# Attention scores with the query halves kept in their own partitions: three products on 64-row tiles, two head pairs at a time

## The chip, the cores and the metric

The kernel runs on one core of one Trainium2 chip. The metric is the device time of one launch in microseconds (us). The kernel before takes 839.48 us, the median of three runs (838.78 to 839.79).

## The reference, cut to what matters

The input `x` is (8, 512, 512): eight rows of 512 tokens and 512 features. Each row attends to its own 64 context tokens (16 heads of 32 features), is projected and added back, and then goes through a gated feed-forward layer with ternary weights and quantised activations. Only the scores are touched by the change.

```python
q = _nan_clean(proj(hs, Wq, bq, S))
k = _nan_clean(proj(at, Wk, bk, T))
v = _nan_clean(proj(at, Wv, bv, T))
scale = max(math.sqrt(HD), 1e-08)
scores = jnp.einsum('bhsd,bhtd->bhst', q, k) / scale
scores = jnp.clip(scores, -50.0, 50.0)
...
scores = jnp.where(attend, scores, -10000.0)
scores = jnp.clip(scores, -50.0, 50.0)
probs = jax.nn.softmax(scores, axis=-1)
...
ctx = jnp.einsum('bhst,bhtd->bhsd', probs, v)
```

Queries and keys are float32 numbers held as two float16 parts, a high one (the number rounded) and a low one (what is left), so that TensorE can multiply them as float16.

## The kernel before

**The work.** A row of `x` is four tiles of 128 tokens. `body(b, ...)` does the feed-forward of row b and, in its gaps, the attention of row a = b + 1 and the layer norm of row c = b + 2. It is called for b = -1 to 8: b = 1 to 5 are a hardware loop, the others straight code. "Body 3" below is the call with b = 3. Scores are computed in the eight bodies b = -1 to 6, once each. Inside a body, t runs over the four token tiles: at t = 0 the queries of row a are made, at t = 1 its scores, at t = 2 the weighted values, and at t = 3 the projection begins. The order on each engine is written out by hand and every dependence is a semaphore: a wait holds up all that stands behind it on its engine.

**Queries, t = 0.** On TensorE (PE), `query(m)` (L1447) makes 128 features, that is four heads, with twelve matmuls in one of the two PSUM banks `psA`. On ScalarE (ACT), `query(m)` (L729) copies the bank, scaled, to `q_whole` (L740), and then writes the high part in two copies (L743, L744): partitions 0 to 63 (two heads) into slot 2m of `q_parts` and partitions 64 to 127 (the other two) into slot 2m + 1, each staying in its partitions. On VectorE (DVE), `q_low` (L959) writes the low part of each half (L964, L965) into the other half of the partitions of the same slot. A slot has thus 64 rows of high and 64 rows of low parts of the same two heads.

**Scores, t = 1.** `scores(j)` on PE (L1459) makes a pair of heads with two matmuls of 128 rows by 512 tokens (L1470, L1471): high keys against both parts of the query, then low keys against both. The keys of a row stand in `kcur`, loaded from a scratch tensor by `load_keys` (L416) with eight DMAs; in each slot they are laid out block by block with zeros, so that one head's keys fill 64 of the 128 output rows. On ACT, `exps` (L746) turns each finished bank into exponentials (L749). The banks alternate:

```python
if j >= 2:
    wait(pe, p_ready, a, j - 1)
```

so that the product of one pair is made in one bank while ACT reads the other. Between scores, PE does parts of `down` (L1430), the output matrix of the feed-forward of the tile before, by the table `BETWEEN_SCORES` (L1655): 12 of its 16 matmuls (L1435). The last 4 stand behind `project`. ACT rounds the next tile's input (L709) between the second and the third exponential.

**Behind the scores.** PE does two transposes (L1410, L1378) and the projection (L1444, thirteen matmuls), whose bank is free once the last exponential is done. ACT copies the transposed layer norm (`h_high`, L679) behind its last exponential. DVE then does `h_low` (L970), four clips of the exponentials (`bound`, L1077), the statistics of the projection (L1018), and, at t = 2, the gated products (L983, L988) with the attention output (L1083, L1088, L1096) between them.

Of the kernel before, what the change touches and what calls it, by code (L numbers as in the profile page):

```python
# [17 lines left out]
F16 = mybir.dt.float16  # L18
# [6 lines left out]
P = 128  # L25
# [34 lines left out]
def build(nc, x, ctx_in, mask, g_x, g_f, Wq, bq, Wk, bk, Wv, bv, Wo, bo, ln_g, ln_b, res_scale,  # L60
# [18 lines left out]
    with es:  # L79
# [47 lines left out]
        q_parts = room(6).bitcast(F16).rearrange("p (j s) -> p j s", j=NPAIR)  # L127
# [49 lines left out]
        kcur = sb("kcur", [P, 2 * NPAIR, 2 * T], F16)  # L177
# [105 lines left out]
        k_loaded = per_row("keys_loaded", 16 * 2 * HPC)  # L283
# [112 lines left out]
        def _(sp):  # L396
# [19 lines left out]
            def load_keys(row):  # L416
                wait_alone(sp, s_met_sp, sc_done, row - 1, NPAIR)
                for i in range(HPC):
                    for q in range(2):
                        e = i % 2  # L420
                        head = HD * (2 * q + e)
                        sp.dma_start(kcur[HD * i:HD * (i + 1), q::2, e * T:(e + 1) * T],
                                     k_dram[head:head + HD, :, row, :]).then_inc(k_loaded.sem, 16)
# [223 lines left out]
        def _(act):  # L647
# [34 lines left out]
            def body(b, prev, ffn, att, pre):  # L682
# [46 lines left out]
                def query(m):  # L729
                    wait(act, q_done, a, m + 1)  # L730
                    if b is FIRST and m == 0:
                        act.wait_ge(s_vmax, 1)
                    if ffn and not prev and m == 0:
                        act.wait_ge(s_wabs, 3 * W_CHUNKS)
                    if m < 2:
                        wait(act, c_tr, b, NT)
                    else:
                        wait(act, ql_ready, a, m - 1)
                    whole = q_whole[:, m % 2, :]
                    A.activation(whole, psA[(m + 1) % 2][:], ACT.Identity, scale=down_q[:, 0:1],  # L740
                                 bias=bq_c[:, m:m + 1]).then_inc(qT_ready.sem, 1)
                    wait(act, qT_ready, a, m + 1)
                    A.copy(q_parts[0:P // 2, 2 * m, :], whole[0:P // 2, :])  # L743
                    A.copy(q_parts[P // 2:, 2 * m + 1, :], whole[P // 2:, :]).then_inc(qh_ready.sem, 1)  # L744
# [135 lines left out]
        def _(dve):  # L880
# [78 lines left out]
            def q_low(row, m):  # L959

                wait(dve, qh_ready, row, m + 1)
                one, other = slice(0, P // 2), slice(P // 2, P)
                whole = q_whole[:, m % 2, :]
                V.tensor_tensor(q_parts[other, 2 * m, :], whole[one, :], q_parts[one, 2 * m, :], ALU.subtract)  # L964
                V.tensor_tensor(q_parts[one, 2 * m + 1, :], whole[other, :], q_parts[other, 2 * m + 1, :],  # L965
# [377 lines left out]
        def _(pe):  # L1343
# [39 lines left out]
            def body(b, prev, ffn, att, pre):  # L1383
# [75 lines left out]
                def scores(j):  # L1459
                    if j == 0:  # L1460
                        wait(pe, ql_ready, a, KC)
                        wait(pe, k_loaded, a, 16 * 2 * HPC)
                        if pre:
                            wait(pe, lo_ready, c, 1)
                    if j == 1:
                        wait(pe, d_ready, b, 3)
                    if j >= 2:
                        wait(pe, p_ready, a, j - 1)

                    M.matmul(psA[(j + 1) % 2][:], kcur[:, j, :], q_parts[:, j, :], start=True, stop=False)  # L1470
                    M.matmul(psA[(j + 1) % 2][:], kcur[:, NPAIR + j, :], q_parts[:, j, :],  # L1471
                             start=False, stop=True).then_inc(sc_done.sem, 1)
# [45 lines left out]
                for t in range(NT):  # L1518
# [46 lines left out]
                    if att and t == 1:  # L1565
                        if out_w_now:
                            pe.wait_ge(s_wcopy, 3 * W_GROUPS)
                        for j in range(NPAIR):
                            scores(j)
                            if finish and j in BETWEEN_SCORES:  # L1570
                                down(*last, BETWEEN_SCORES[j])
# [83 lines left out]
BETWEEN_SCORES = {1: range(0, 5), 2: range(5, 6), 3: range(6, 9), 4: range(9, 10), 5: range(10, 11), 6: range(11, 12)}  # L1655
AFTER_SCORES = 12
# [23 lines left out]
```

## Time and profile before

| | |
|---|---|
| median of 3 runs | 839.48 us (838.78 to 839.79) |
| the profiled execution | 841.52 us, span 839.7 us |
| mean granted TensorE clock | 0.970 of full |
| DMA | 50.90 MB, 61 GB/s |
| instructions | 14590 |

The span runs from the first to the last instruction. One body of the loop takes some 88 us of it. The profile gives for each engine the time in which an instruction ran; on PE, matmuls follow each other before the earlier one has ended, so the distance between two starts is what one costs in a stream and its duration is what one costs alone.

### The profile page before, as it was taken

Reading aid. Unit: us, or ns where it says so; the run is one execution under the profiler, and the core shown is the slowest. Engines: PE = TensorE matmul, PEld = TensorE weight load, DVE = VectorE, ACT = ScalarE, POOL = GpSimd, SP = SyncE. Lnnn points to the kernel's source line nnn. Section 1 sums busy time; section 2 is a strip of 40 time slices with the busy share of each in tenths; the row PEclk is TensorE's granted clock in tenths of the full one; section 3 lists DMA queues with packets and bytes.
Section 4 is the critical chain, followed back from the end, with each engine's and each line's share of the span. In section 5 each row is a group of like instructions: output and inputs, shape, how many; then the busy total and the mean of one; then the engine's idle time right before and its main releaser. Section 6 shows DMA issues by size and latency. Waiting matters only on the chain.

```text
span 839.7 us, 14590 instructions
## 1 busy us (share of the span) xinstructions
PE 750.2 (89%) x4886; PEld 384.6 (46%) x4886; DVE 697.7 (83%) x1412; ACT 534.0 (64%) x693; POOL 240.2 (29%) x427
## 2 busy tenths in 40 slices
PE   4695658969999999999999999999999999999995
PEld 4442344434544454445444544454445444454442
DVE  6778876898889888888988988988888888779982
ACT  4447858767557755784578557855676556745563
POOL 4101003221333324232433333314422332223431
PEclk9898768999999999999999999999999999999998
DMA  8572345101030103011211121111111020001000
GB/s 275 192 261 64 130 165 170 26 14 39 2 95 10 42 26 77 17 37 37 56 37 37 37 52 42 37 37 42 51 37 37 17 52 26 26 2 51 13 26 26
DMA packets 51663, 50.90 MB, mean 61 GB/s; under 512 B 30877, under 2 KB 30877, under 8 KB 50857
## 3 DMA queue, kind: packets, MB, share of 16 engines
q1 hardware_dynamic: 51624, 50.42, 19.2%
q8 instruction: 21, 0.34, 0.2%
q14 instruction: 18, 0.14, 0.1%
HBM read 39.91 MB, written 10.50 MB: 60 GB/s over the span
## 4 chain that ended last, share of the span: by engine, by line
PE 45%; DVE 31%; issue 11%; ACT 10%; POOL 1%; DMA 1%; DVEq 0%; POOLq 0%; ACTq 0%
PE psum L1444 14%; PE psum L1399 13%; PE psum L1435 7%; DVE arena L988 4%; DVE psum L983 3%; ACT arena L749 2%; DVE arena L1088 2%; PE psum L1402 2%; PE psum L1427 2%; PE psum L1378 2%; DVE xmax L1060 1%; DVE arena L1096 1%; PE psum L1470 1%; DVE stats L1048 1%; DVE arena L922 1%
## 5 line engine op out<-in xcount | busy, mean ns | idle before, releaser
L1399 PE MATMUL psum<-ternary,xqT 128*128 128x512 f16 x1024 | 261.3, 379 | 2.8 <-DVE xqT L1009 2.6
L554 POOL TENSOR_TENSOR rstd<-var_e,minus_half 128x1 f32<-128x1 f32 x64 | 40.0, 625 | 406.5 <-DVE var_e L1028 263.9
L1399 PEld LDWEIGHTS psum<-ternary,xqT 128*128 128x128 f16 x1024 | 96.3, 98 | 108.3 <-DVE xqT L1009 3.5
L1435 PE MATMUL psum<-ternary,arena 128*128 128x512 f16 x512 | 128.0, 383 | 1.2 <-ACT arena L726 1.2
L693 ACT ACTIVATE arena<-psum,dequant 128x512 f32<-128x512 f32 x128 | 87.2, 682 | 43.2 <-PE psum L1402 42.8
L983 DVE SCALAR_TENSOR_TENSOR psum<-psum,dequant,valb_b 128x512 f32<-128x512 f32 x128 | 96.3, 752 | 20.2 <-PE psum L1399 19.7
L988 DVE TENSOR_TENSOR arena<-psum,arena 128x512 f32<-128x512 f32 x128 | 88.5, 692 | 20.8 <-ACT arena L693 17.1
L1444 PE MATMUL psum<-wo_hi,arena 128*128 128x512 f16 x256 | 84.4, 392 | 2.5 <-DVE arena L1096 1.9
L1444 PE MATMUL psum<-arena,wq_hi 128*128 128x512 f16 x256 | 77.5, 385 | 7.1 <-ACT arena L740 7.1
L726 ACT ACTIVATE arena<-psum,round_c 128x1024 f16<-128x1024 f16 x64 | 71.3, 1114 | 19.1 <-PE psum L1427 18.7
L701 ACT ACTIVATE arena<-arena,round_c,hscale 128x1024 f32<-128x1024 f32 x64 | 75.9, 1236 | 4.6 <-DVE hscale L1004 4.4
L992 DVE TENSOR_REDUCE hmax<-arena 128x1 f32<-128x1024 f32 x64 | 77.6, 1213 | 0.7
L1435 PEld LDWEIGHTS psum<-ternary,arena 128*128 128x128 f16 x512 | 48.9, 99 | 57.4 <-ACT arena L726 4.4
L1444 PE MATMUL psum<-wo_lo,arena 128*128 128x512 f16 x128 | 50.1, 391 | 0.0
L586 POOL TENSOR_TENSOR arena<-arena 128x512 f32<-128x512 f32 x32 | 42.2, 1319 | 25.2 <-ACT arena L721 25.2
L1444 PE MATMUL psum<-arena,wq_lo 128*128 128x512 f16 x128 | 49.2, 384 | 0.0
L1402 PE MATMUL psum<-bias_parts,inv_rows 128*128 128x512 bf16 x128 | 48.5, 379 | 0.0
L749 ACT ACTIVATE arena<-psum,scur 128x512 f32<-128x512 f32 x64 | 46.5, 775 | 1.2 <-PE psum L1471 0.5
L714 ACT CAST inv_rows<-psum 128x128 bf16<-128x128 f32 x32 | 8.6, 269 | 57.7 <-DVE xqT L1009 57.7
L740 ACT ACTIVATE arena<-psum,bq_c,down_q 128x512 f32<-128x512 f32 x32 | 24.9, 777 | 30.4 <-PE psum L1444 28.9
L709 ACT ACTIVATE arena<-x_both,round_c,xscale 128x512 f32<-128x512 f32 x32 | 25.9, 810 | 27.8 <-DVE xscale L1070 27.7
L1492 PE MATMUL psum<-vcur,arena 128*64 128x66 f32 x1024 | 38.3, 229 | 5.8 <-DVE delta L1033 4.4
(181 smaller groups left out, 1348.7 us busy)
## 6 DMA issues: line engine op xcount, KB each, us to landing
arena<-in_x SPq DMA_DIRECT2D x64, 256.0 KB, 2.7
out<-arena SPq DMA_DIRECT2D x32, 256.0 KB, 2.0
arena<-in_L_ffn_gate_w SPq DMA_DIRECT2D x4, 1024.0 KB, 10.0
arena<-in_L_ffn_out_w SPq DMA_DIRECT2D x3, 1024.0 KB, 9.6
ternary<-in_L_ffn_val_w SPq DMA_DIRECT2D x2, 1024.0 KB, 10.2
kcur<-k_scratch SPq DMA_DIRECT2D x64, 32.0 KB, 2.2
ternary<-in_ctx SPq DMA_DIRECT2D x1, 1024.0 KB, 5.4
ternary<-in_L_xattn_Wk SPq DMA_DIRECT2D x1, 1024.0 KB, 8.0
```

The source lines that it names most:

```text
L586: G.tensor_tensor(resid[:, t, :], resid[:, t, :], y_part[:, t % 2, :], ALU.add).then_inc(y_ready.sem, 1)
L693: A.activation(gs[:, t % 2, n * CW:(n + 1) * CW], psG[n % 2], ACT.Silu, scale=dequant[:, t, 0:1]).then_inc(silu_done.sem, 1)
L701: A.activation(gs[:, t % 2, cols], gs[:, t % 2, cols], ACT.Identity, scale=hscale[:, t:t + 1], bias=round_c[:, 0:1]).then_inc(hq_ready.sem, 1)
L726: A.activation(hidT[:, h * FC // 2:(h + 1) * FC // 2, :].rearrange("p k n -> p (k n)"), half(psO), ACT.Identity, bias=round_c[:, 1:2]).the ...
L749: A.activation(probs[:, j, :], psA[(j + 1) % 2][:], ACT.Exp, scale=scur[:, 0:1], bias=scur[:, 1:2]).then_inc(p_ready.sem, 1)
L983: V.scalar_tensor_tensor(out=psV[n % 2], in0=psV[n % 2], scalar=dequant[:, t, 1:2], in1=valb_b[:, n * CW:(n + 1) * CW], op0=ALU.mult, op1= ...
L988: V.tensor_tensor(part, psV[n % 2], part, ALU.mult).then_inc(hid_ready.sem, 1)
L992: V.tensor_reduce(hmax[:, t, h:h + 1], gs[:, t % 2, h * F // 2:(h + 1) * F // 2], AX, ALU.max, apply_absolute_value=True).then_inc(hm_read ...
L1399: ins = M.matmul(ps[:], xqT[:, t % 2, k, :], w[:, k, cols], start=(k == 0), stop=(w is wv and k == KC - 1))
L1402: ins = M.matmul(ps[:], inv_rows[:, t % 2, :], bias_parts[:, cols], start=False, stop=True)
L1435: ins = M.matmul(psO[:], hidT[:, k, :], wo2[:, k, :], start=(k == 0), stop=(k == FC - 1))
L1444: ins = M.matmul(ps[:], lhsT, rhs, start=(n == 0), stop=(n == len(pairs) - 1))
```

## The change

`q_parts` becomes four-dimensional (part, m, token): all 128 partitions of the high part lie in one place and all of the low part in another, so nothing crosses partitions. ACT writes the high part with one copy for each m, DVE the low part with one subtraction. `kcur` is laid out in the same way, with four DMAs for each row of `x`. `scores(m)` takes the place of two calls of `scores(j)`: six matmuls, each on 64 of the 128 rows, in turn on the lower half (two heads, bank `psA[1]`) and on the upper half (the next two, bank `psA[0]`): high keys by high query, high by low, low by high. The product of the low parts is left out.

```diff
-        q_parts = room(6).bitcast(F16).rearrange("p (j s) -> p j s", j=NPAIR)
+        q_parts = room(6).bitcast(F16).rearrange("p (two m s) -> p two m s", two=2, m=KC)
...
-        kcur = sb("kcur", [P, 2 * NPAIR, 2 * T], F16)
+        kcur = sb("kcur", [P, 2, KC, 2 * T], F16)
...
                 for i in range(HPC):
-                    for q in range(2):
-                        e = i % 2
-                        head = HD * (2 * q + e)
-                        sp.dma_start(kcur[HD * i:HD * (i + 1), q::2, e * T:(e + 1) * T],
-                                     k_dram[head:head + HD, :, row, :]).then_inc(k_loaded.sem, 16)
+                    e, head = i % 2, slice(HD * i, HD * (i + 1))
+                    sp.dma_start(kcur[head, :, :, e * T:(e + 1) * T].rearrange("p two m t -> p (two m) t"),
+                                 k_dram[head, :, row, :]).then_inc(k_loaded.sem, 16)
...
                     wait(act, qT_ready, a, m + 1)
-                    A.copy(q_parts[0:P // 2, 2 * m, :], whole[0:P // 2, :])
-                    A.copy(q_parts[P // 2:, 2 * m + 1, :], whole[P // 2:, :]).then_inc(qh_ready.sem, 1)
+                    A.copy(q_parts[:, 0, m, :], whole).then_inc(qh_ready.sem, 1)
...
                 wait(dve, qh_ready, row, m + 1)
-                one, other = slice(0, P // 2), slice(P // 2, P)
-                whole = q_whole[:, m % 2, :]
-                V.tensor_tensor(q_parts[other, 2 * m, :], whole[one, :], q_parts[one, 2 * m, :], ALU.subtract)
-                V.tensor_tensor(q_parts[one, 2 * m + 1, :], whole[other, :], q_parts[other, 2 * m + 1, :],
+                V.tensor_tensor(q_parts[:, 1, m, :], q_whole[:, m % 2, :], q_parts[:, 0, m, :],
                                 ALU.subtract).then_inc(ql_ready.sem, 1)
...
-                def scores(j):
-                    if j == 0:
+                def scores(m):
+                    if m == 0:
                         wait(pe, ql_ready, a, KC)
-                        wait(pe, k_loaded, a, 16 * 2 * HPC)
+                        wait(pe, k_loaded, a, 16 * HPC)
                         if pre:
                             wait(pe, lo_ready, c, 1)
-                    if j == 1:
                         wait(pe, d_ready, b, 3)
-                    if j >= 2:
-                        wait(pe, p_ready, a, j - 1)
-
-                    M.matmul(psA[(j + 1) % 2][:], kcur[:, j, :], q_parts[:, j, :], start=True, stop=False)
-                    M.matmul(psA[(j + 1) % 2][:], kcur[:, NPAIR + j, :], q_parts[:, j, :],
-                             start=False, stop=True).then_inc(sc_done.sem, 1)
+                    else:
+                        wait(pe, p_ready, a, 2 * m)
+
+                    for n, (of_k, of_q) in enumerate(((0, 0), (0, 1), (1, 0))):
+                        for e in range(2):
+                            pair = slice(e * 2 * HD, (e + 1) * 2 * HD)
+                            ins = M.matmul(psA[(e + 1) % 2][:], kcur[pair, of_k, m, :], q_parts[pair, of_q, m, :],
+                                           start=(n == 0), stop=(n == 2))
+                            if n == 2:
+                                ins.then_inc(sc_done.sem, 1)
...
-BETWEEN_SCORES = {1: range(0, 5), 2: range(5, 6), 3: range(6, 9), 4: range(9, 10), 5: range(10, 11), 6: range(11, 12)}
-AFTER_SCORES = 12
+BETWEEN_SCORES = {0: range(0, 5), 1: range(5, 10), 2: range(10, 15)}
+AFTER_SCORES = 15
```

How the instructions stand, at two places. The first is PE in body 0 at t = 1, from the first product of the scores on (L1470 and L1471 are the two products of a pair, L1435 is `down`; `exp_ready` is the semaphore `p_ready`). Before:

```order
L1470 MATMUL psum<-arena,kcur 128x512 [waits keys_loaded,hT_low_ready,query_low_ready,weight_copied]
L1471 MATMUL psum<-arena,kcur 128x512
L1470 MATMUL psum<-arena,kcur 128x512 [waits delta_ready]
L1471 MATMUL psum<-arena,kcur 128x512
L1435 MATMUL psum<-ternary,arena 128x512 [waits hidT_ready]
L1435 MATMUL psum<-ternary,arena 128x512 x4
L1470 MATMUL psum<-arena,kcur 128x512 [waits exp_ready]
L1471 MATMUL psum<-arena,kcur 128x512
L1435 MATMUL psum<-ternary,arena 128x512
L1470 MATMUL psum<-arena,kcur 128x512 [waits exp_ready]
L1471 MATMUL psum<-arena,kcur 128x512
L1435 MATMUL psum<-ternary,arena 128x512 x3
```

In the changed kernel, from the same place to the transposes (L1466 is the product, L1429 is `down`, L1404 the first transpose):

```order
L1466 MATMUL psum<-arena,kcur 128x512 [waits hT_low_ready,keys_loaded,delta_ready,query_low_ready,weight_copied]
L1466 MATMUL psum<-arena,kcur 128x512 x5
L1429 MATMUL psum<-ternary,arena 128x512 [waits hidT_ready]
L1429 MATMUL psum<-ternary,arena 128x512 x4
L1466 MATMUL psum<-arena,kcur 128x512 [waits exp_ready]
L1466 MATMUL psum<-arena,kcur 128x512 x5
L1429 MATMUL psum<-ternary,arena 128x512 x5
L1466 MATMUL psum<-arena,kcur 128x512 [waits exp_ready]
L1466 MATMUL psum<-arena,kcur 128x512 x5
L1429 MATMUL psum<-ternary,arena 128x512 x5
L1466 MATMUL psum<-arena,kcur 128x512 [waits exp_ready]
L1466 MATMUL psum<-arena,kcur 128x512 x5
```

The groups that wait for exponentials are three instead of six, and each stands for two pairs and waits for the exponentials of both pairs before it. Fifteen `down` matmuls stand in the gaps instead of twelve.

The second place is DVE in body 0 at t = 0, where the low parts of the query are made (L964 and L965), between the work of the feed-forward (L983, L988, L992) and of a weight's clipping (L922). Before:

```order
L992 TENSOR_REDUCE hmax<-arena 128x1
L964 TENSOR_TENSOR arena<-arena 64x512
L965 TENSOR_TENSOR arena<-arena 64x512
L983 SCALAR_TENSOR_TENSOR psum<-psum,dequant,valb_b 128x512
L988 TENSOR_TENSOR arena<-psum,arena 128x512
L922 TENSOR_SCALAR arena<-arena 128x2048
L964 TENSOR_TENSOR arena<-arena 64x512
L965 TENSOR_TENSOR arena<-arena 64x512
```

In the changed kernel (L959 is the low part, L986 is the reduction, L977 and L982 the feed-forward, L919 the clipping):

```order
L986 TENSOR_REDUCE hmax<-arena 128x1
L959 TENSOR_TENSOR arena<-arena 128x512
L977 SCALAR_TENSOR_TENSOR psum<-psum,dequant,valb_b 128x512
L982 TENSOR_TENSOR arena<-psum,arena 128x512
L919 TENSOR_SCALAR arena<-arena 128x2048
L959 TENSOR_TENSOR arena<-arena 128x512
```

One instruction on 128 partitions stands where two on 64 stood, and nothing else has moved.

## Rows read from the trace of the kernel before

**Rows 1.** The page: busy time of the engines, us (share of the span).
```profile
PE 750.2 (89%) x4886; PEld 384.6 (46%) x4886; DVE 697.7 (83%) x1412; ACT 534.0 (64%) x693; POOL 240.2 (29%) x427
```
**Rows 2.** Body 3 in five stretches: busy us of each engine, granted clock, DMA.
```profile
413.80:451.00 37.20, 37.20 (x203) 18.27 (x202) 32.58 (x68) 26.33 (x36) 11.67 (x17) 1.00 0.16 48
451.00:459.10 8.10, 7.92 (x40) 3.03 (x37) 7.00 (x16) 7.96 (x11) 3.75 (x9) 1.00 0.00 0
...
465.65:484.00 18.35, 17.30 (x209) 11.04 (x210) 17.16 (x38) 8.03 (x13) 5.68 (x11) 1.00 0.12 43
```
**Rows 3.** Timeline, scores of body 3, ACT and DVE: start, us, engine, line.
```profile
451.31 1.28 ACT L749 ACT_TABLE_LOAD   x1
452.61 1.45 ACT L749 ACTIVATE arena<-psum,scur 128x512 f32<-128x512 f32 x2
453.95 0.81 ACT L709 ACTIVATE arena<-x_both,round_c,xscale 128x512 f32<-128x512 f32 x1
454.66 4.40 ACT L749 ACTIVATE arena<-psum,scur 128x512 f32<-128x512 f32 x6
459.20 0.59 ACT L679 CAST arena<-psum 128x512 f16<-128x512 f32 x1
...
459.82 0.69 DVE L970 TENSOR_TENSOR arena<-psum,arena 128x512 f16<-128x512 f32 x1 [0.84 <-ACT arena L679]
```
**Rows 4.** Timeline of the same stretch, PE and its weight loads.
```profile
451.27 0.38 PE L1470 MATMUL psum<-arena,kcur 128*128 128x512 f16 x1
451.49 0.38 PE L1471 MATMUL psum<-arena,kcur 128*128 128x512 f16 x1
...
453.44 0.10 PEld L1470 LDWEIGHTS psum<-arena,kcur 128*128 128x128 f16 x1 [0.56 <-ACT arena L749]
```
**Rows 5.** Groups by form: busy us, mean ns of one, idle before.
```profile
L965 DVE TENSOR_TENSOR arena<-arena 64x512 f16<-64x512 f32 x32 | 22.0, 687 | 0.4
L970 DVE TENSOR_TENSOR arena<-psum,arena 128x512 f16<-128x512 f32 x32 | 21.9, 684 | 8.5 <-ACT arena L679 8.5
L744 ACT CAST arena<-arena 64x512 f16<-64x512 f32 x32 | 19.7, 615 | 0.4
L749 ACT ACTIVATE arena<-psum,scur 128x512 f32<-128x512 f32 x64 | 46.5, 775 | 1.2 <-PE psum L1471 0.5
```
**Rows 6.** The chain that ended last, in body 0: start, us, engine, line.
```profile
149.87 0.62 ACT arena L744
...
156.72 0.68 DVE arena L964
157.42 0.69 DVE arena L965
...
198.89 0.86 PE psum L1435 x4
```
**Rows 7.** Timeline of body -1, where the clock is low; ACT and PE.
```profile
84.40 0.62 ACT L744 CAST arena<-arena 64x512 f16<-64x512 f32 x1
...
95.07 0.63 PE L1471 MATMUL psum<-arena,kcur 128*128 128x512 f16 x1
95.49 0.63 PE L1470 MATMUL psum<-arena,kcur 128*128 128x512 f16 x1
...
95.80 1.57 ACT L749 ACTIVATE arena<-psum,scur 128x512 f32<-128x512 f32 x2
101.58 1.44 ACT L749 ACTIVATE arena<-psum,scur 128x512 f32<-128x512 f32 x2
```
**Rows 8.** Timeline, PE: matmuls on 64 output columns (L1492) and on whole tiles.
```profile
465.65 1.16 PE L1492 MATMUL psum<-vcur,arena 128*64 128x66 f32 x32 [0.75 <-DVE delta L1033]
52.33 10.55 PE L1627 MATMUL psum<-ternary 128*128 128x512 f32 x24
```
**Rows 9.** Timeline of body 0: the table load waits for the first score.
```profile
188.12 1.28 ACT L749 ACT_TABLE_LOAD   x1 [1.95 <-PE psum L1471]
```
**Rows 10.** Timeline of the DMA queue: issue of the keys for body 3.
```profile
410.13 3.94 SPq L422 DMA_DIRECT2D kcur<-k_scratch  x6
```

More of the change, by code:

```diff
@@ L282, in build @@
         xt_loaded = [per_row(f"xt{i}_loaded", 16 * NT // 2) for i in range(2)]
-        k_loaded = per_row("keys_loaded", 16 * 2 * HPC)
+        k_loaded = per_row("keys_loaded", 16 * HPC)
         v_loaded = per_row("values_loaded", 16 * 2)
@@ L1567, in body @@
                             pe.wait_ge(s_wcopy, 3 * W_GROUPS)
[L1568 to L1571, printed above, removed]
+                        for m in range(KC):
+                            scores(m)
+                            if finish and m in BETWEEN_SCORES:
+                                down(*last, BETWEEN_SCORES[m])
                     if finish and not (att and t == 1):
```

## The prediction

> **What bounds the kernel now.** I read the busy times, then one body of the loop in stretches, then the timeline inside the stretch that the change touches, and last the chain of waits for the bodies that differ. PE is busy for 89% of the span and DVE for 83% [rows 1]; such averages do not say which of the two a saving must come from. The stretches do [rows 2]. From 413.8 to 451.0 us (queries, first gate products) PE is busy for all of 37.20 us, with DVE at 32.58 and ACT at 26.33: a PE stretch. From 451.0 to 459.1 (the scores) ACT is busy for 7.96 of 8.10 us. PE shows 7.92 there too, but its busy time counts a matmul to its end; its weight loads show real stops, such as 0.56 us before a score, released by ACT's exponential [rows 4]. From 465.65 to 484.0 DVE carries the time, 17.16 of 18.35.
>
> The scores are the place to look at closely [rows 3]: a table load at 451.31, two exponentials, the rounding at 453.95, six exponentials in one run of 4.40 us from 454.66, the copy L679 at 459.20. ACT never stops. It does not, because the banks alternate: PE makes pair j + 1 while ACT reads pair j. And all that follows waits for this run: DVE stands idle for 0.84 us before L970 at 459.82, released by L679, so DVE has no backlog to hide a later end in, and the projection needs the last exponential as well.
>
> **The change, part by part.** Differences within 0.2% (1.7 us) I call the same.
>
> *High and low parts of the queries.* ACT loses one of two copies for each m, 615 ns; DVE one of two subtractions, 687 ns. The ones that stay take 128 partitions instead of 64, at the same 512 elements in each: the 128-partition subtraction L970 takes 684 ns [rows 5], so they cost no more than one half did. That is 32 of each, 22.0 us of DVE and 19.7 us of ACT in all. In bodies 1 to 6 it lies under PE's unbroken 37 us: **0**. The cover is PE, and no other work is queued late at its end, since ACT and DVE both wait for something in the score stretch. In body 0 the weights are still being clipped on DVE and the chain runs through both subtractions of all four m (156.72 and 157.42 are the first two) and through one copy at 149.87 [rows 6]: -4 x 0.69 - 0.62 = **-3.4 us**, at least 0 if another engine takes over at once. In body -1, two ACT copies (84.40 is one) and one subtraction stand in the same kind of chain ahead of the scores [rows 7]: -0.62 x 2 - 0.69 = **-1.9 us**.
>
> *Key loads.* Four DMAs instead of eight. Those for body 3 are issued from 410.13 [rows 10] and read at 451.27 [rows 4]: 41 us early. **0**, either way.
>
> *The scores.* Two products of a pair start 0.22 us apart [rows 4], so 16 full products are 3.5 us of PE. The new 24 on 64 rows are 12 x 0.22 = 2.6 us if the two halves of the array work at once, and 5.2 us if not. No row shows 64-row tiles. The nearest are 64-column ones: 32 float32 matmuls of 66 columns start and end in 1.16 us, 0.036 us each, while 24 of 512 columns take 10.55 us, 0.44 us each, which for 66 columns would be 0.057 us [rows 8]. Two such tiles do overlap, so I take the halves as concurrent and keep the serial price as the other end.
>
> What matters is the wait. `scores(m)` needs **both** banks, so it needs both exponentials of the two pairs before. PE cannot make the next scores under an exponential any more, and ACT stands still from the end of one pair of exponentials until the fifth of six products has ended. From exponential to PE 0.05 us (452.61 + 0.78 = 453.39, load at 453.44 [rows 3 to 5]); two steps of 0.22 to the fifth start; 0.38 to its end [rows 4]; 0.05 back to ACT: 0.91 us. Walking through body 3:
> - exponentials 0 and 1 start at 452.61 as before, since the table load covers the longer first group (451.27 + 0.43 + 0.38 = 452.08), and end at 454.06;
> - 2 and 3: 454.06 + 0.91 = 454.97, not 454.66. The rounding covers the rest. They end at 456.42;
> - 4 and 5: start at 457.33, end at 458.78;
> - 6 and 7: start at 459.69, end at **461.14**, against 454.66 + 4.40 = 459.06 before.
>
> That is **+2.1 us a body**. Queued behind it are h_low, the clips and the statistics on DVE, L679 and the quantisation on ACT, and the projection on PE; all of them move. For seven bodies (0 to 6): **+14.6**. In bodies 0 and 6 the table load itself waits for the first score [rows 9], which now ends one step later: **+0.4** together. In body -1 the clock is at its lower level, steps are 0.42 us and a product 0.63 [rows 7], and the layer norm stands ahead of the last two exponentials. The run from 95.80 to 103.02 (101.58 + 1.44) would grow by 0.4 before its first exponential, by some 1.5 at the second group, 0.9 at the third (clock back up) and little at the fourth, less 0.35 of waits that it has already: **+2.4**.
>
> *`down`.* Three more of its matmuls lie in gaps where PE waits for ACT: 5 x 0.22 = 1.1 us after 0.65 us of scores end before the exponentials do (1.45 + 0.91 from one group to the next). Behind the projection 1 is left instead of 4. In bodies 1 to 6 DVE comes there from its clips and is last: 0. In body 0 the four are on the chain [rows 6]: **-0.6**.
>
> **Sum:** -3.4 - 1.9 + 14.6 + 0.4 + 2.4 - 0.6 = **+11.5 us**, against a profiled execution of 841.5 us (span 839.7). The median of the runs is 2.0 us under that execution; the difference carries over, so 839.5 + 11.5 = **851.0 us**.
>
> Two rules speak on the score term. The rows gave a gap by the wait alone. The Trainium skill, TensorEngine Tiling (Array Packing), PSUM Bottleneck, says that tiling speeds up TensorE and not the emptying of PSUM; the 7.96 of 8.10 us of ACT [rows 2] agree, and by that rule alone the change would give 0 in the score stretch and not a loss, a result of 833.6. The same page, Key Properties, says that a change of tiling mode drains TensorE; no row here shows such a change between row tilings. As an estimate, a drain of 0.16 us (a product's 0.38 less its step of 0.22) at each group would be hidden where PE waits anyway.
>
> **Rivals.**
> 1. *The halves run one after the other.* The fifth product then starts 0.86 us after the first, and each gap is 1.34 us: per body +0.4 at the second group and +0.43 at each of the last two, 3.4 us instead of 2.1; +0.9 more in bodies 0 and 6, +2.5 in body -1. Sum: 11.5 + 9.1 + 0.9 + 2.5 = +24, **863.5 us**. For it: nothing in the rows shows two row tiles at once. Against: the column tiles overlap [rows 8]. 0.17.
> 2. *The relief is worth more than the gap* (faster). If the late part of DVE's work in a body began earlier by its 2.75 us for four subtractions, the loss of 2.1 would turn into -0.65 a body: -4.6 for seven, and with -3.4, -1.9, -0.6, +0.4 and +2.4 about **832 us**. It decides where DVE has no idle time between t = 0 and L970. DVE's 32.58 of 37.20 us and its 0.84 us wait speak against it [rows 2, 3]. 0.04.
> 3. *The score stretch costs nothing* and only the relief is left, as the emptying rule has it: PE would have to start a group ahead of the second exponential, which the wait forbids. -3.4 - 1.9 - 0.6 = **833.6 us**. 0.03.
> 4. *The clock falls.* PE now stops for some 0.5 to 1 us three times in the stretch. If the granted clock, 1.00 in all of body 3 [rows 2], dropped to its lower level for the 2.8 us of the projection in each of seven bodies, that adds 2.8 x 7 = 20 us: **871 us**. PE was busy the stretch before and is again right after. 0.03.
>
> **How the numbers follow.** My forecast has 0.73 and its own range is 848 to 855: body 0's relief may be 0 instead of 3.4, and the terms of body -1 are rough by 2 us. The predicted time is its time. To hold 8 in 10 the range goes down to 846 and up over the serial case to 865. Faster: rivals 2 and 3, 0.07. The same: 0.02, a mixture of a smaller gap and more relief. Slower: 0.91.
>
> **What would show it.** In the changed profile: 32 whole-width copies near 0.62 us and 32 subtractions near 0.69; in each looped body ACT idle twice by about 0.9 us before an exponential, released by PE, with one run of six split into three pairs; pairs of products starting within a few hundredths of a microsecond of each other (rival 1: 0.22 apart); L679 of body 3 2.1 us later after the table load than now (7.9 us); the loop's bodies at 90 us instead of 88, and bodies -1 and 0 together shorter or level. The forecast is wrong if ACT still runs its exponentials without a stop, or if the stretch is longer and the body is not.

## The result, and the profile after

| | before | after |
|---|---|---|
| median of the runs, us | 839.63 (838.78 to 840.45, 4 runs) | 849.73 (848.55 to 850.84, 4 runs) |
| profiled execution, us | 841.5 | 848.55 |
| its span, us | 839.7 | 846.8 |
| mean granted clock of the span | 0.97 | 0.97 |

The ratio is 1.012, with a 95% interval from 1.0101 to 1.0139. The changed kernel is slower by 10.1 us, and its time lies 1.3 us under the predicted 851.0.

The page of the changed kernel, its busy times (to set beside [rows 1]) and two groups, then the groups by form (beside [rows 5]; columns: busy us, mean ns of one, idle time before and what ended it):

```profile
PE 742.3 (88%) x4888; PEld 382.9 (45%) x4950; DVE 667.4 (79%) x1380; ACT 511.1 (60%) x661; POOL 237.8 (28%) x427
L746 ACT ACTIVATE arena<-psum,scur 128x512 f32<-128x512 f32 x64 | 46.3, 773 | 17.0 <-PE psum L1466 16.9
L1466 PE MATMUL psum<-arena,kcur 64*128 64x512 f16 x192 | 26.9, 387 | 19.3 <-ACT arena L746 16.7
```

```profile
L959 DVE TENSOR_TENSOR arena<-arena 128x512 f16<-128x512 f32 x32 | 23.5, 739 | 0.0
L741 ACT CAST arena<-arena 128x512 f16<-128x512 f32 x32 | 19.8, 618 | 1.0
```

DVE lost 30 us of busy time and ACT 23, and the kernel is slower. The reason stands in the idle column of L746: the exponentials, which waited 1.2 us in all before, now wait 17.0, for the scores; and the scores wait 16.7 of their 19.3 for the exponentials. The two engines take turns where they used to overlap. The timeline of ACT in the score stretch of body 3 shows it (beside [rows 3]; columns: start us, us, engine, line, count, in brackets the idle time before the group and what ended it):

```profile
451.14 1.28 ACT L746 ACT_TABLE_LOAD   x1
452.44 1.45 ACT L746 ACTIVATE arena<-psum,scur 128x512 f32<-128x512 f32 x2
453.78 0.81 ACT L707 ACTIVATE arena<-x_both,round_c,xscale 128x512 f32<-128x512 f32 x1
454.80 1.45 ACT L746 ACTIVATE arena<-psum,scur 128x512 f32<-128x512 f32 x2 [0.21 <-PE psum L1466]
457.15 1.44 ACT L746 ACTIVATE arena<-psum,scur 128x512 f32<-128x512 f32 x2 [0.91 <-PE psum L1466]
459.51 1.45 ACT L746 ACTIVATE arena<-psum,scur 128x512 f32<-128x512 f32 x2 [0.91 <-PE psum L1466]
461.11 0.58 ACT L677 CAST arena<-psum 128x512 f16<-128x512 f32 x1
```

One run of six has become three pairs. From the first exponential to the end of the last it is 460.96 - 452.44 = 8.52 us, against 459.06 - 452.61 = 6.45 before: +2.07. The same stretch on PE, beside [rows 4]:

```profile
451.20 0.82 PE L1466 MATMUL psum<-arena,kcur 64*128 64x512 f16 x6
451.95 1.25 PE L1429 MATMUL psum<-ternary,arena 128*128 128x512 f16 x5
453.94 0.82 PE L1466 MATMUL psum<-arena,kcur 64*128 64x512 f16 x6 [0.74 <-ACT arena L746]
454.69 1.25 PE L1429 MATMUL psum<-ternary,arena 128*128 128x512 f16 x5
456.30 0.82 PE L1466 MATMUL psum<-arena,kcur 64*128 64x512 f16 x6 [0.35 <-ACT arena L746]
```

Six products start and end in 0.82 us, which is two steps of 0.22 and one duration of 0.38: three pairs side by side. Even the five `down` matmuls between two groups leave PE standing for 0.35 us. DVE waits longer for the copy behind the last exponential, 1.40 us instead of 0.84 [rows 3]:

```profile
461.72 0.69 DVE L964 TENSOR_TENSOR arena<-psum,arena 128x512 f16<-128x512 f32 x1 [1.40 <-ACT arena L677]
```

**Where the time went.** The two profiled executions, piece by piece; the marks are the table loads L749/L746 ahead of the exponentials, which start at 188.12, 275.50, 363.51, 451.31, 539.08, 626.84 and 714.80 before, and at 182.17, 271.65, 361.40, 451.14, 540.89, 630.63 and 720.89 after (bodies 0 to 6).

| piece | before, us | after, us | difference | by the prediction's terms |
|---|---|---|---|---|
| start to the rounding L662/L660, ahead of any changed work | 67.75 | 65.86 | -1.9 | 0 |
| from there to the first exponential of body -1 | 28.05 | 24.45 | -3.6 | -1.9 |
| from it to the copy L679/L677 behind the last | 7.30 | 9.68 | +2.4 | +2.4 |
| from there to the table load of body 0 | 85.02 | 82.18 | -2.8 | -3.4 + 0.2 |
| table load of body 0 to that of body 6 | 526.68 | 538.72 | +12.0 | 6 x 2.1 + 0.2 - 0.6 |
| from there to the end of the span | 124.9 | 125.9 | +1.0 | +2.1 |

Together +7.1, the difference of the spans. The first row is no effect of the change; without it the sum is +9.0. The medians of the runs differ by 10.1, so this pair of executions shows about 3 us less than the runs do; the table is for the pieces, not for the total.

### The profile page after: what moved, and what is told of

The parts are those of the page before. It is cut to its first block, busy times and chain, and to the rows that moved or that the text cites. A ratio compares the mean times of both kernels' runs of the same rounds, so it can differ in the third digit from the quotient of the medians.

```text
span 846.8 us, 14525 instructions
## 1 busy us (share of the span) xinstructions
PE 742.3 (88%) x4888; PEld 382.9 (45%) x4950; DVE 667.4 (79%) x1380; ACT 511.1 (60%) x661; POOL 237.8 (28%) x427
## 4 chain that ended last, share of the span: by engine, by line
PE 41%; DVE 32%; ACT 13%; issue 11%; POOL 1%; DMA 1%; DVEq 0%; POOLq 0%; another core or an unknown queue 0%; ACTq 0%; SPq 0%
PE psum L1438 13%; PE psum L1393 12%; PE psum L1429 6%; ACT arena L746 4%; DVE arena L982 4%; DVE psum L977 4%; PE psum L1466 3%; DVE arena L1082 2%; DVE hmax L986 2%; PE psum L1372 2%; DVE xmax L1054 1%; PE psum L1421 1%; DVE arena L1071 1%; ACT arena L699 1%; DVE arena L1090 1%
## 5 line engine op out<-in xcount | busy, mean ns | idle before, releaser
L1393 PE MATMUL psum<-ternary,xqT 128*128 128x512 f16 x1024 | 261.3, 379 | 5.5 <-DVE xqT L1003 1.5
L1393 PEld LDWEIGHTS psum<-ternary,xqT 128*128 128x128 f16 x1024 | 96.4, 98 | 107.0 <-DVE arena L982 3.1
L1429 PE MATMUL psum<-ternary,arena 128*128 128x512 f16 x512 | 124.8, 383 | 1.6 <-ACT arena L724 1.2
L977 DVE SCALAR_TENSOR_TENSOR psum<-psum,dequant,valb_b 128x512 f32<-128x512 f32 x128 | 96.2, 752 | 29.4 <-PE psum L1393 29.4
L982 DVE TENSOR_TENSOR arena<-psum,arena 128x512 f32<-128x512 f32 x128 | 88.5, 691 | 21.4 <-ACT arena L691 17.6
L986 DVE TENSOR_REDUCE hmax<-arena 128x1 f32<-128x1024 f32 x64 | 77.6, 1213 | 0.7
L1429 PEld LDWEIGHTS psum<-ternary,arena 128*128 128x128 f16 x512 | 47.2, 99 | 61.3 <-issue 11.1
L746 ACT ACTIVATE arena<-psum,scur 128x512 f32<-128x512 f32 x64 | 46.3, 773 | 17.0 <-PE psum L1466 16.9
L738 ACT ACTIVATE arena<-psum,bq_c,down_q 128x512 f32<-128x512 f32 x32 | 24.8, 776 | 43.7 <-PE psum L1438 43.2
L1489 PE MATMUL psum<-vcur,arena 128*64 128x66 f32 x1024 | 40.0, 236 | 8.9 <-DVE delta L1027 7.5
L1489 PEld LDWEIGHTS psum<-vcur,arena 128*64 128x64 f32 x1024 | 35.7, 148 | 22.0 <-issue 14.8
L558 POOL TENSOR_TENSOR arena<-arena,beta_b 128x512 f32<-128x512 f32 x32 | 44.4, 1388 | 0.0
L1466 PE MATMUL psum<-arena,kcur 64*128 64x512 f16 x192 | 26.9, 387 | 19.3 <-ACT arena L746 16.7
```

What stands on the lines that cost most here:

```text
L746: A.activation(probs[:, j, :], psA[(j + 1) % 2][:], ACT.Exp, scale=scur[:, 0:1], bias=scur[:, 1:2]).then_inc(p_ready.sem, 1)
L977: V.scalar_tensor_tensor(out=psV[n % 2], in0=psV[n % 2], scalar=dequant[:, t, 1:2], in1=valb_b[:, n * CW:(n + 1) * CW], op0=ALU.mult, op1= ...
L982: V.tensor_tensor(part, psV[n % 2], part, ALU.mult).then_inc(hid_ready.sem, 1)
L986: V.tensor_reduce(hmax[:, t, h:h + 1], gs[:, t % 2, h * F // 2:(h + 1) * F // 2], AX, ALU.max, apply_absolute_value=True).then_inc(hm_read ...
L1393: ins = M.matmul(ps[:], xqT[:, t % 2, k, :], w[:, k, cols], start=(k == 0), stop=(w is wv and k == KC - 1))
L1429: ins = M.matmul(psO[:], hidT[:, k, :], wo2[:, k, :], start=(k == 0), stop=(k == FC - 1))
```

## The experiments

Each kernel ran beside the kernel before on the same chip. That took 840.31 us (839.06 to 842.86) beside four of them (the wait alone, the first with four banks, pair by pair, the halves) and 840.91 (838.47 to 842.45) beside the other four. Line numbers shift by a few from kernel to kernel.

### Is it the wait? The old products under the new wait

The kernel before, two 128-row products a pair, made to wait for both exponentials of the two pairs before:

```diff
-                    if j >= 2:
-                        wait(pe, p_ready, a, j - 1)
+                    if j >= 2 and j % 2 == 0:
+                        wait(pe, p_ready, a, j)
```

> The kernel before, with one thing changed: an even pair of heads waits for the exponentials of both pairs before it (p_ready, j) instead of for its own bank. No 64-row tile, no relief of DVE or ACT. Gap theory: at pairs 4 and 6 ACT stops for 0.05 + 0.22 + 0.38 + 0.05 = 0.70 us where it ran on with an overlap of 0.05, at pair 2 the rounding covers all but 0.1 us: +1.6 us a body, seven bodies +11.2, body -1 some +1.5: about 852 us. Rival, that the loss of the change comes from the tiled products (their drains, their issue) or from the table of down: no change, 839.6 us.

Measured: 853.48 us (851.59 to 854.09), 1.0157 (1.0141 to 1.0173). ACT in body 3:

```profile
459.67 1.45 ACT L749 ACTIVATE arena<-psum,scur 128x512 f32<-128x512 f32 x2
461.82 1.45 ACT L749 ACTIVATE arena<-psum,scur 128x512 f32<-128x512 f32 x2 [0.70 <-PE psum L1471]
463.96 1.45 ACT L749 ACTIVATE arena<-psum,scur 128x512 f32<-128x512 f32 x2 [0.70 <-PE psum L1471]
```

Nothing but a wait was changed, no product, copy or subtraction, and the kernel is slower by 13 us, more than the change itself. The gap is one product step shorter than the change's 0.91, because a pair is ready after two products. The loop's period is 89.22 us against 87.78: +1.44. So of the change's +2.07 a body, 1.44 is the wait and 3 x 0.21 = 0.63 the third product, one step at each of the three later groups.

### And the other way: the new products without the wait

The change with four banks for the scores. Pairs 2, 3, 6 and 7 go to the two banks of the gate products, which are free in that stretch in all bodies but body -1:

```diff
+        def scores_bank(b, j):
+            return (psG if j // 2 % 2 and b is not FIRST else psA)[(j + 1) % 2]
...
-                    else:
+                    elif b is FIRST:
                         wait(pe, p_ready, a, 2 * m)
+                    elif m == 1:
+                        wait(pe, silu_done, b, 2 * NCH)
+                    else:
+                        wait(pe, p_ready, a, 2 * m - 2)
```

> The changed kernel with the scores of m = 1 and 3 in the two banks of the gate (free by then) instead of in the same two, except in body -1: m = 1 waits for the last silu, m = 2 and 3 for the exponentials of m = 0 and 1. The products stay six at a time on both halves. Gap theory: ACT's exponentials run without a stop from the first to the last in bodies 0 to 6 as before the change, 6.45 us from the first start to the last end against 8.52 now: 849.7 - 7 x 2.1 = 835 us, under both kernels. Rival, that something else than the gap holds the stretch (PE's drains, DVE): 845 to 850 us.

Measured: 836.56 us (835.58 to 837.93), 0.9952 (0.9938 to 0.9966). ACT in body 3:

```profile
450.25 2.89 ACT L750 ACTIVATE arena<-psum,scur 128x512 f32<-128x512 f32 x4
453.64 1.45 ACT L750 ACTIVATE arena<-psum,scur 128x512 f32<-128x512 f32 x2 [0.49 <-PE psum L1474]
```

The gap of 0.21 and the first of 0.91 are gone, one of 0.49 is left ahead of the last two exponentials, and the loss has turned into a gain. The rest is a matter of the table: three groups of five `down` matmuls (1.1 us each) now keep PE from running ahead. With the table of `down` spread over all four groups of scores:

```diff
-BETWEEN_SCORES = {0: range(0, 5), 1: range(5, 10), 2: range(10, 15)}
-AFTER_SCORES = 15
+BETWEEN_SCORES = {0: range(0, 6), 1: range(6, 10), 2: range(10, 12), 3: range(12, 14)}
+AFTER_SCORES = 14
```

> The version with four banks, and a table of down that brings the last scores forward: 6, 4, 2 and 2 of down's matmuls behind the four groups, 2 left. In its trace ACT still stops for 0.49 us before the last two exponentials of a body, because ten down matmuls stand ahead of the last group on PE. With that gap gone: seven bodies x 0.49 = 3.4 us less than with the first table, about 833 us against 840.3 before. If the stop had another cause it stays, 836.6 us.

Measured: **834.22 us** (832.70 to 835.22), 0.992 (0.9904 to 0.9936): faster than both kernels. ACT in body 3:

```profile
446.27 1.45 ACT L750 ACTIVATE arena<-psum,scur 128x512 f32<-128x512 f32 x2
447.61 0.81 ACT L711 ACTIVATE arena<-x_both,round_c,xscale 128x512 f32<-128x512 f32 x1
448.31 4.23 ACT L750 ACTIVATE arena<-psum,scur 128x512 f32<-128x512 f32 x6
```

The unbroken run of six is back, 4.23 us instead of 4.40. The loop's period is 87.50 us against 87.78 before: 0.17 of it is the shorter run, and 0.11 is what the halved kernel below shows for the relief in the loop. So without the wait, and with this table, the change is worth 6.7 us by the medians. The spans of the two profiled executions differ by 7.2; 1.2 of that stands ahead of any changed work. Of the other 6.0, 4.0 lie between there and the table load of body 0, 1.6 from that to the table load of body 6, and 0.4 behind it. Whether the shorter run of exponentials would come to the kernel before as well, if it had four banks, was not tried.

### Half of the wait: pair by pair

The change with the scores asked for pair by pair (three products on one half of the array, waiting for the exponential before last, as before the change), and with the old table of `down`:

```diff
-                    else:
-                        wait(pe, p_ready, a, 2 * m)
+                    if j >= 2:
+                        wait(pe, p_ready, a, j - 1)
```

> The changed kernel with the scores made pair by pair in turn in the two banks, each waiting for its own bank only, three products of 64 rows one after the other, and the down table of the kernel before. The halves of the array then work in turn. Gap theory: from the end of an exponential to the next one in the same bank 0.05 + 0.43 + 0.38 + 0.05 = 0.91 us, in which the other bank's exponential runs 0.73: a gap of some 0.2 us at five pairs, 1.0 us a body instead of 2.1, and less in body -1: about 849.7 - 8 = 842 us. Rival, that the two halves at once are what saves time and the wait costs little: slower than the change, over 852 us.

Measured: 846.11 us (845.80 to 847.07), 1.0066 (1.005 to 1.0082): a miss by 4 us. Five lines of PE and three of ACT say why:

```profile
449.83 0.83 PE L1467 MATMUL psum<-arena,kcur 64*128 64x512 f16 x6
450.59 1.25 PE L1429 MATMUL psum<-ternary,arena 128*128 128x512 f16 x5
...
454.48 0.82 PE L1467 MATMUL psum<-arena,kcur 64*128 64x512 f16 x3
455.23 0.39 PE L1429 MATMUL psum<-ternary,arena 128*128 128x512 f16 x1
455.55 0.82 PE L1467 MATMUL psum<-arena,kcur 64*128 64x512 f16 x3
```

```profile
455.34 0.78 ACT L746 ACTIVATE arena<-psum,scur 128x512 f32<-128x512 f32 x1 [0.73 <-PE psum L1467]
456.41 0.78 ACT L746 ACTIVATE arena<-psum,scur 128x512 f32<-128x512 f32 x1 [0.30 <-PE psum L1467]
457.48 0.78 ACT L746 ACTIVATE arena<-psum,scur 128x512 f32<-128x512 f32 x1 [0.30 <-PE psum L1467]
```

A single pair's three products take as long as six of two pairs, 0.82 us, and what follows them starts 0.75 us after the first. With one `down` matmul behind them, 0.32 us more, PE comes to a new pair every 1.07 us, and between these groups it does not stop for ACT: here PE sets the pace, and ACT's 0.78 + 0.30 a pair only follows. The expectation had counted the wait for the bank and not PE's own time. The three `down` matmuls ahead of pair 4 hold that pair back further, 0.73. What the array gains by working in halves is had only where both halves have a free bank at the same moment.

### Does the third product cost its step? A fourth one

The change with the product of the low parts put back:

```diff
-                    for n, (of_k, of_q) in enumerate(((0, 0), (0, 1), (1, 0))):
+                    for n, (of_k, of_q) in enumerate(((0, 0), (0, 1), (1, 0), (1, 1))):
```

> The changed kernel with the product of the two low parts put back: eight matmuls for each m instead of six, on both halves in turn. Gap theory: each gap between pairs of exponentials grows by one step of 0.22 us, from 0.91 to 1.13 and from 0.21 to 0.43: +0.65 us a body, eight bodies +5.2, and 0.4 more where the table load waits for the first score. Against the kernel before +10.1 + 5.6, about 855.8 us. Rival, that PE's work and not the gap is what costs: PE has 8 x 0.22 = 1.7 us more a body, mostly in time in which it waits, so no change, or the whole +14 us, 864 us, if it stood on PE's path.

Measured: 856.79 us (855.76 to 858.31), 1.0193 (1.0175 to 1.0211). ACT and PE in body 3:

```profile
460.16 1.45 ACT L746 ACTIVATE arena<-psum,scur 128x512 f32<-128x512 f32 x2 [0.43 <-PE psum L1466]
462.74 1.45 ACT L746 ACTIVATE arena<-psum,scur 128x512 f32<-128x512 f32 x2 [1.13 <-PE psum L1466]
```

```profile
461.67 1.04 PE L1466 MATMUL psum<-arena,kcur 64*128 64x512 f16 x8 [0.35 <-ACT arena L746]
```

Each gap grew by one step: 0.43, 1.13 and 1.13, where it was 0.21, 0.91 and 0.91; eight products take 1.04. The loop's period rises by 0.65, three steps. Rival 1 of the prediction would have shown 0.43 a gap.

### Are the halves at work together only because they alternate?

The change with each group's products in another order, three on the lower half, then three on the upper:

```diff
-                    for n, (of_k, of_q) in enumerate(((0, 0), (0, 1), (1, 0))):
-                        for e in range(2):
+                    for e in range(2):
+                        for n, (of_k, of_q) in enumerate(((0, 0), (0, 1), (1, 0))):
```

> The changed kernel with the six products in another order: three on the lower half of the array, then three on the upper. Same waits. If two halves run at once only because the order alternates, the group now takes 1.46 us instead of 0.82. Gap theory: the first bank of the group is finished by its third product at 0.43 + 0.38 = 0.81 us, as before, and the second at 1.46, before the first exponential has ended (0.81 + 0.05 + 0.73), so ACT's gaps stay at 0.91 and 0.21 and the time stays at 849.7 to 850.5 us. PE's group and five down matmuls then fill 2.4 us, the whole distance of 2.36 between two groups, so up to +0.1 us at two gaps of a body, +1.4 in all. Rival, that concurrency of the halves is what the time hangs on: +0.65 us at each of three gaps, +14 us, 864 us.

Measured: 849.21 us (848.24 to 851.58), 1.011 (1.0087 to 1.0132), the change's own time within the noise. PE in body 3:

```profile
454.67 0.83 PE L1466 MATMUL psum<-arena,kcur 64*128 64x512 f16 x6 [0.73 <-ACT arena L746]
455.43 1.25 PE L1429 MATMUL psum<-ternary,arena 128*128 128x512 f16 x5
```

In a row the six would have taken 5 x 0.22 + 0.38 = 1.48 us, and the next matmul would have started 1.3 us after the first; it starts after 0.76. So three products that stand behind three others in the program ran beside them. The first line of the pair-by-pair kernel shows the same, since its pairs 0 and 1 are also written one after the other.

### What is the relief worth? Half-width copies and subtractions in the change

The change with the copy and the subtraction of each m cut into two halves again, as many instructions as before the change:

```diff
-                    A.copy(q_parts[:, 0, m, :], whole).then_inc(qh_ready.sem, 1)
+                    A.copy(q_parts[0:P // 2, 0, m, :], whole[0:P // 2, :])
+                    A.copy(q_parts[P // 2:, 0, m, :], whole[P // 2:, :]).then_inc(qh_ready.sem, 1)
```

The subtraction in `q_low` is cut in the same way.

> The changed kernel with the high and the low part of the query again written by two instructions of 64 partitions each. If the relief is worth what was forecast (3.4 us in body 0, 1.9 in body -1, nothing in the others): 849.7 + 5.3 = 855.0 us. If it is worth more, because body -1 came 5.5 us earlier in the changed trace: up to 858. If it is worth nothing: 849.7 us. In bodies 1 to 5 the distance from one table load to the next stays at 89.8 us under the first two.

Measured: 858.54 us (856.52 to 859.11), 1.0208 (1.0191 to 1.0224). By the medians the relief is worth 8.8 us, or 8.1 if each kernel is set against the runs of the kernel before that were taken beside it, and not 5.3. The period of the loop is 89.86 against 89.75: the cover that the prediction named, PE's 37 us, holds but for 0.11. Most of the relief sits in the two other bodies. The way from the rounding L660 to the first exponential of body -1 is 94.42 - 66.23 = 28.19 us, as before the change (28.05), against 24.45; and from the copy L677 of body -1 to the table load of body 0 it is 190.12 - 105.41 = 84.71, near the 85.02 of before, against 82.18. These are 3.7 and 2.5 us. The spans of the two profiled executions differ by 9.9. Of the rest, 1.3 is the score stretch of body -1, 10.99 us here against 9.68; that is not the relief, since two kernels that have the relief show 10.88 (the first with four banks) and 10.99 (the one with 12 `down` matmuls, below), with the clock at 0.50 in most of it. 0.4 stands ahead of any changed work, 0.8 from the table load of body 0 to that of body 6, and 1.2 behind that, with no cause shown. ACT in body -1, of the kernel before, of the change, and of this one:

```profile
82.96 0.78 ACT L740 ACTIVATE arena<-psum,bq_c,down_q 128x512 f32<-128x512 f32 x1 [0.97 <-DVE arena L965]
...
93.23 0.59 ACT L679 CAST arena<-psum 128x512 f16<-128x512 f32 x1 [1.98 <-PE psum L1378]
```

```profile
80.00 0.76 ACT L738 ACTIVATE arena<-psum,bq_c,down_q 128x512 f32<-128x512 f32 x1
...
87.92 0.58 ACT L677 CAST arena<-psum 128x512 f16<-128x512 f32 x1 [1.16 <-PE psum L1372]
...
90.31 1.44 ACT L746 ACTIVATE arena<-psum,scur 128x512 f32<-128x512 f32 x2
```

```profile
81.31 0.78 ACT L738 ACTIVATE arena<-psum,bq_c,down_q 128x512 f32<-128x512 f32 x1 [0.85 <-DVE arena L962]
...
91.43 0.59 ACT L677 CAST arena<-psum 128x512 f16<-128x512 f32 x1 [1.82 <-PE psum L1375]
```

Whole-width work takes away three things: the wait of ACT for the subtractions (0.97), two copies, and some 0.8 us of the wait for the transposes behind them. PE comes to these sooner after its last work (it had stood still for 1.06 us in the change, for 2.46 us in the other two) and has its full clock: the stretches of body -1 of the kernel before, of the change and of this one (length, PE, weight loads, DVE, ACT, POOL; then the granted clock, DMA) show 0.50, 1.00 and 0.50 there.

```profile
90.00:93.00 3.00, 2.70 (x20) 2.26 (x20) 2.82 (x5) 1.25 (x2) 1.32 (x3) 0.50 0.01 3
```

```profile
87.00:90.00 3.00, 1.51 (x18) 0.90 (x15) 2.04 (x6) 2.08 (x2) 0.75 (x3) 1.00 0.01 3
```

```profile
90.00:93.00 3.00, 1.51 (x12) 1.14 (x11) 2.04 (x5) 1.57 (x2) 0.00 (x0) 0.50 0.00 0
```

### What is the new table of `down` worth?

The change with 12 of its matmuls between the scores, as before, and four behind the projection:

```diff
-BETWEEN_SCORES = {0: range(0, 5), 1: range(5, 10), 2: range(10, 15)}
-AFTER_SCORES = 15
+BETWEEN_SCORES = {0: range(0, 5), 1: range(5, 9), 2: range(9, 12)}
+AFTER_SCORES = 12
```

> The changed kernel with 12 of down's 16 matmuls between the scores, as before the change, instead of 15. The forecast has the three in question at 0 in bodies 1 to 5 and at 0.6 us in body 0; the changed trace shows 0.3 in body 0, given back later, and 0.6 in body 6: +0.5 to +1 us, not to be told from the change itself. Rival, that the other table is a part of the loss or the gain: 2 us or more in either direction.

Measured: 851.30 us (850.08 to 852.08), 1.0122 (1.0103 to 1.0142), which cannot be told from the change by the time alone. By the table loads the loop has the same period (453.13 to 542.90, 89.77 against 89.75). Body 6 is where it counts. The statistics of DVE there, in this kernel and in the change:

```profile
735.80 0.70 DVE L1012 BATCH_NORM_STATS2 stats<-psum 128x6 f32<-128x512 f32 x1 [1.30 <-PE psum L1438]
745.05 0.68 DVE L1042 BATCH_NORM_STATS2 stats<-x_both 128x6 f32<-128x512 f32 x1
```

```profile
733.77 0.70 DVE L1012 BATCH_NORM_STATS2 stats<-psum 128x6 f32<-128x512 f32 x1 [1.30 <-remote]
742.38 0.68 DVE L1042 BATCH_NORM_STATS2 stats<-x_both 128x6 f32<-128x512 f32 x1
```

9.25 us with four `down` matmuls behind the projection, 8.61 with one: three steps. In body 0 the period does not show them, 89.50 us in this kernel and 89.48 in the change.

## Why the prediction was right, point by point

- **The gap.** 0.91 us was worked out from a semaphore's 0.05, two steps and one duration; the trace has 0.91 and 0.21. A body was to grow by 2.1 and grew by 2.07 in its score stretch and by 1.97 in the loop's period. The 0.1 between the two is the relief: the halved kernel has the same 8.52 us in the stretch and a period 2.08 us over the one before. The wait alone (1.44 of it), a fourth product (0.65 more) and four banks with the spread table (nothing left) each move it as the formula says. That is the term that carries the result, and it is shown.
- **The halves are concurrent.** 0.82 us for six; rival 1 is out. So is rival 3: the stretch grew by 2.07 us, where the emptying rule as the prediction used it gave no loss. That rule comes from the Trainium skill, TensorEngine Tiling (Array Packing), PSUM Bottleneck: tiling speeds up TensorE and not the emptying of PSUM. The trace agrees that the emptying itself is as before (exponentials busy for 46.5 us before, 46.3 after); what was lost is its overlap with the products. The Trainium skill, TensorEngine Tiling (Array Packing), Gotcha 1: PSUM Pressure, says that different row tiles write to different banks, so that row tiling raises the pressure on PSUM. This case agrees and puts a price on it: two pairs at once took both banks, nothing was left to alternate with, and each later group shows a gap of 0.91 us. With four banks and the spread table the kernel came to 834.22, close to the 833.6 of rival 3 but by other terms: in the profiled executions body -1 has -3.6 and, with its two banks, still +2.4, body 0 -2.8, and the rest -2.0.
- **No relief in the loop.** 0 was forecast; 0.11 us a body is what the halved kernel shows. Rival 2 is out.
- **Body -1.** The relief was put at -1.9 and measured -3.6: a term of the sum that was too small. The prediction counted the two copies (1.24) and one subtraction. A copy gave more than its duration: on ACT it is 1.27 us from the first copy of an m to what follows (83.77 to 85.04) before, and 0.52 (80.79 to 81.31) after, 0.75 less and not 0.62. The chain held ACT's wait of 0.97, which ended with the second subtraction, and, behind the copies, transposes that PE did at a granted clock of 0.50 after a stop of 2.46 us; in the change the stop is 1.06 and the clock 1.00. By pieces: from DVE's shift (80.98 before, 79.09 after) to the start of L740/L738 1.98 became 0.91; from there to the end of the second rounding 8.29 became 6.76; from that to L679/L677 1.98 became 1.16; the last 0.2 stands behind it. The +2.4 of its score stretch came out as +2.4, but not by the steps named, so the size is luck: the clock was at 1.00 until 96 us, the gaps were 0.91, 0.91 and 0.85, the exponentials took 1.9 us longer in all, and the rest is a wait of the copy L677 for transposes, 0.54. In the halved kernel, at 0.50 there, a gap is 1.55, near the 1.5 forecast.
- **Body 0.** -3.4 for the relief and +0.2 for the table load were forecast, -2.8 was measured for both. The halved kernel puts the relief alone at 2.5. The size is near that of four subtractions (2.76); why it is less than 3.4 is not shown.
- **`down`.** -0.6 was placed in body 0 and 0 in bodies 1 to 6; both places are wrong and the sum is right. In body 0 PE came to the weighted values earlier by three steps and waited there for DVE instead, 1.03 us where it had waited 0.38; in body 6 the 0.64 reached the end. PE in body 0, before and after:

```profile
202.08 1.16 PE L1492 MATMUL psum<-vcur,arena 128*64 128x66 f32 x32 [0.38 <-DVE delta L1033]
```

```profile
198.21 1.16 PE L1489 MATMUL psum<-vcur,arena 128*64 128x66 f32 x32 [1.03 <-DVE delta L1027]
```

- **The clock** did not fall in the loop, and rival 4 is out: 1.00 in the score stretch of body 3 although PE stood still there three times (same columns as above):

```profile
451.00:461.05 10.05, 8.05 (x51) 2.81 (x50) 6.71 (x16) 7.89 (x11) 3.74 (x8) 1.00 0.00 0
```

The sum was +11.5 and should be set, for this pair of executions, against +9.0: 1.7 us of the difference are body -1's relief, 0.6 are `down` in body 6, some 0.5 in the same last piece has no cause shown, and body 0 takes back 0.4. The medians differ by 10.1. Why the two profiled executions differ by less than the medians was not settled. Two things point at chance: the piece ahead of any changed work lies between 65.86 us (the change) and 67.75 us (the kernel before) in the ten kernels, and these two are its ends; and the same score stretch of body -1 took 9.68 us in the change and 9.69, 10.88 and 10.99 in three other kernels, by how long the clock stayed at 1.00. So the mechanism is shown, while the closeness of 851.0 to 849.73 is partly luck: errors of 1.7 and 0.6 us stand against an unexplained difference between executions.

## What to carry to other kernels

Before joining two pieces of work on one engine, count the banks that they fill against the banks that the reader empties: a wait for two buffers out of two turns an overlap into a turn-taking, and costs one hand-over a group, whatever the engine saves. Price it as semaphore + steps + duration + semaphore from existing rows; here that gave 0.91 us exactly. And look for free banks elsewhere in the same stretch before accepting the loss: two idle ones turned 10.1 us slower into 3.8 us faster, and with the work between the scores spread anew into 6.7 us faster.

## What the runs showed that was not expected

- Three 64-row products on the upper half ran beside three on the lower half although they stood behind them in the program: six in 0.83 us, the next matmul 0.76 us after the first, in two kernels. Which half each start belongs to the trace does not say.
- Going from 128-row matmuls to 64-row ones and back takes about 0.1 us each way. In the kernel before, the first score product starts 0.86 us after the first of the four matmuls L1399 ahead of it (450.41 to 451.27), that is four steps and nothing more. In the changed kernel it starts 0.53 us after the first of the last two matmuls L1393 (450.67 to 451.20, the line below), two steps and 0.10, and the first `down` matmul starts 0.75 us after the first of the six products, three steps and 0.09 more. The prediction's estimate was 0.16. In the change this is covered: the gaps come out at 0.91 without it. Pair by pair it is paid each time: 3 x 0.22 + 0.09 + 0.22 + 0.10 = 1.07.

```profile
450.67 0.59 PE L1393 MATMUL psum<-ternary,xqT 128*128 128x512 f16 x2
```

- A subtraction on DVE took 1.76 us instead of 0.68 while an addition of POOL ran beside it, which was longer as well, 2.26 us instead of a median of 1.28. The kernel before has such a subtraction in each of bodies 1 to 6, 1.52 to 1.55 us (one of them 256.21 to 257.76, beside the addition from 255.93 to 257.20); the change has only this one, so its timing alone took six of them away. In both kernels the subtraction ends 0.55 to 0.56 us behind the end of the addition, as if it had waited for it. That both have two inputs from the same memory and keep each other waiting is a guess; it wasn't tried. DVE and POOL in body 0 of the changed kernel:

```profile
155.56 2.26 POOL L558 TENSOR_TENSOR arena<-arena,beta_b 128x512 f32<-128x512 f32 x1
...
156.61 1.76 DVE L959 TENSOR_TENSOR arena<-arena 128x512 f16<-128x512 f32 x1
```
